# A two-layer graph kernel: column passes of 512 contiguous columns, moving rows laid 544 bytes apart, and other first steps

## The reference

```python
deg = max(sum(adj != 0, axis=-1), 1)
d = rsqrt(deg)
pooled = (d * (adj + I) * d) @ x + x          # layer 0
x = layernorm(x + relu(pooled @ W + b))
# layer 1
a = sigmoid([adj @ x, x] @ Wa.T + ba); g = sigmoid([adj @ x, x] @ Wb.T + bb)
h = x @ W_sa
scores = (h @ a_l)[:, None] + (h @ a_r)[None, :]
e = where(adj != 0, exp(-leaky_relu(scores, 0.01)), 0)
x_a = (e / (sum(e, axis=1) + 1e-5)) @ h
x_b = adj @ (x @ W_gcnb) + b_gcnb
out = layernorm(x + sigmoid(a * x_a + g * x_b))
```

## Time and profile before

| | us |
|---|---|
| median of three runs | 945.04 |
| the profiled execution | 944.09 |
| its span (first to last instruction) | 942.3 |
| PE busy | 901.3 (96%) |
| PE weight loads busy | 783.3 (83%) |
| DVE busy | 640.2 (68%) |
| ACT busy | 459.7 (49%) |
| L1148 / L1031 / L1110 busy on PE | 346.5 / 245.9 / 232.4 |

### The profile page before, as it was taken

The page is one execution under the profiler, slowest core; times in us unless marked ns, Lnnn a source line. Parts: engine busy times, 40 slices in busy tenths (PEclk is TensorE's granted clock), DMA queues, the critical chain, the costliest instruction groups (busy, mean ns, idle before and its releaser), DMA issues.

```text
span 942.3 us, 20464 instructions
## 1 busy us (share of the span) xinstructions
PE 901.3 (96%) x7829; PEld 783.3 (83%) x7829; DVE 640.2 (68%) x1432; ACT 459.7 (49%) x642; POOL 87.4 (9%) x139
## 2 busy tenths in 40 slices
PE   7995799999999999979999999999999999999996
PEld 6874688888888888858888888888888888888885
DVE  6576555544554446777998797797797797797762
ACT  2653455455455324655656365365355455455450
POOL 1020212222212210000000000000000000000000
PEclk8998999999999999979999999999999999999999
DMA  9978899999999400102201110111111211101000
GB/s 303 273 239 266 285 308 329 311 306 338 300 312 332 165 18 18 52 1 74 73 19 68 61 49 35 61 40 44 61 30 54 61 27 56 61 22 59 15 24 12
DMA packets 95784, 121.65 MB, mean 129 GB/s; under 512 B 6480, under 2 KB 91504, under 8 KB 91632
## 3 DMA queue, kind: packets, MB, share of 16 engines
q1 hardware_dynamic: 91120, 116.69, 37.8%
q10 hardware_dynamic: 4608, 4.20, 1.3%
HBM read 95.69 MB, written 25.18 MB: 128 GB/s over the span
## 4 chain that ended last, share of the span: by engine, by line
PE 82%; DVE 9%; ACT 3%; issue 3%; DMA 2%; POOL 0%; SPq 0%; DVEq 0%; ACTq 0%; POOLq 0%
PE ps L1148 32%; PE ps L1031 22%; PE ps L1110 20%; PE ps L1066 4%; DVE ec L866 3%; PE ps L1014 3%; DVE em L875 1%; ACT ec L516 1%; ACT em L519 1%; DMA strip<-in_adj_dram 1%; DMA xs<-in_x_dram 1%; DVE y L640 1%; PE ps L1051 1%; PE ps L1003 1%; DVE codes L600 0%
## 5 line engine op out<-in xcount | busy, mean ns | idle before, releaser
L1148 PE MATMUL ps<-fb,em 128*128 128x257 f16 x3072 | 346.5, 275 | 8.1 <-DVE em L875 8.1
L1148 PEld LDWEIGHTS ps<-fb,em 128*128 128x128 f16 x3072 | 301.4, 98 | 50.9 <-issue 8.6
L1031 PE MATMUL ps<-y,codes 128*128 128x257 f16 x2048 | 245.9, 276 | 11.7 <-DVE lnst L766 7.8
L1031 PEld LDWEIGHTS ps<-y,codes 128*128 128x128 fp8e4 x2048 | 201.8, 99 | 44.9 <-DVE lnst L766 8.1
L1110 PE MATMUL ps<-fa,pan 128*128 128x258 f16 x2048 | 232.4, 273 | 0.9 <-DVE slrow L834 0.9
L1110 PEld LDWEIGHTS ps<-fa,pan 128*128 128x128 fp8e4 x2048 | 199.2, 97 | 30.7 <-DVE slrow L834 1.2
L866 DVE SCALAR_TENSOR_TENSOR ec<-slb,sr,pan 128x256 f32<-128x256 f32 x512 | 207.9, 478 | 7.6 <-issue 7.3
L516 ACT ACTIVATE ec<-ec,sc 128x2048 f32<-128x2048 f32 x64 | 127.9, 1999 | 131.1 <-DVE ec L866 131.1
L875 DVE SCALAR_TENSOR_TENSOR em<-ec,em 128x2048 f16<-128x2048 f32 x64 | 146.4, 2287 | 16.6 <-ACT em L519 16.5
L519 ACT ACTIVATE em<-ec 128x2048 f16<-128x2048 f32 x64 | 122.3, 1911 | 8.2
L738 DVE TENSOR_SCALAR lnst<-ps 128x1 f32<-128x1 f32 x32 | 5.0, 157 | 107.9 <-PE ps L1031 107.9
(11 more groups left out here) (99 smaller groups left out, 503.0 us busy)
## 6 DMA issues: line engine op xcount, KB each, us to landing
strip<-in_adj_dram SPq DMA_DIRECT2D x128, 512.0 KB, 6.2
a_scratch<-codes SPq DMA_DIRECT2D x16, 1024.0 KB, 8.4
pan<-a_scratch SPq DMA_DIRECT2D x16, 1024.0 KB, 5.0
x_scratch<-x ACTq DMA_DIRECT2D x32, 128.0 KB, 4.7
x1r<-x_scratch SPq DMA_DIRECT2D x32, 128.0 KB, 2.1
out_dram<-ot SPq DMA_DIRECT2D x32, 128.0 KB, 1.7
xs<-in_x_dram SPq DMA_DIRECT2D x3, 1024.0 KB, 11.0
slb<-sl_scratch SPq DMA_DIRECT2D x16, 128.0 KB, 4.7
```

What stands on the lines that cost most here:

```text
L1031: mm = pe.matmul(ACC(n), codes[:, qq % SLOTS, h, jb, e * P:(e + 1) * P].bitcast(F8), y[:, jb, part, :], start=(jb == 0 and part == 0), sto ...
L1148: mm = pe.matmul(PH(b)[:, 0:HC], em[slot][:, e_part, jb, (b % 2) * P:(b % 2 + 1) * P], fb[:, jb, h_part, :], start=(jb == 0 and e_part + h ...
```

## The change

What it does:

- A pass takes 512 adjacent columns. A strip is now 2 row blocks of 512 columns (2 KB contiguous) instead of 4 of 256 (1 KB), still 512 KB. `strip_at` and `TILES` go; tiles are taken in the order 0, 1, 2, ... Casts read a strip as it lies and write two pieces of the codes (128x2x2x256 instead of 128x1024). Both code panels of a pass are written to DRAM together.
- xs, fa, zf, fb and y have rows of 272 numbers (`ROW`), so every f16 row begins 544 bytes after the one before; the matmuls still take 257 or 258 columns.
- ACT copies z for the first ten tiles (`ZACT`) and DVE only from the eleventh; DVE takes all six maxima of x and `z_scale` ahead of that. y follows by `split_at`: two tiles a step until it has caught up, then one step behind.
- The weight steps of DVE are spread: `weight_column` at t = 18 to 21, `weight_squares` at 22, `weight_norm` at 26, `weight_scale` at 28, `weight_parts` at 29 and 30.
- 16 row blocks of pass 0 go into the z steps instead of 20 (and 24 before the tile-wise rest: `OUTER`). `t_step(0)` stands behind the third output tile of pass 0 and `p_step(0)` behind the fourth.
- Behind the z steps, ACT and DVE take `head` and `normalize` of the first tiles between the casts, two at a time.
- In the first two panels DVE's `low_chunk` follows its `relu_chunk` by two chunks instead of one, through both panels.

```diff
-SJ = 4
-NSTRIP = NPAN * T // SJ
+SJ = 2
+GS = T // SJ
+NSTRIP = NQ * GS
+ZACT = 10
-YLAG = 10
-OUTER = 24
+OUTER = 16
+ROW = 272
-TILES = [2 * q + h * (T // 2) + e for q in range(NQ) for h in range(2) for e in range(2)]
...
-    fa = at("fa", [P, T, 2, GC], F16, O_X)
+    fa = at("fa", [P, T, 2, ROW], F16, O_X)
-    fb = at("fb", [P, T, 2, HC], F16, O_Z)
-    y = at("y", [P, T, 2, YC], F16, O_Y)
+    fb = at("fb", [P, T, 2, ROW], F16, O_Z)
+    y = at("y", [P, T, 2, ROW], F16, O_Y)
...
-                qq, h, g = strip_at(s)
-                c0 = (qq + h * NQ) * PW
-                sp.dma_start(strip[:, s % RING], adj_view[:, g * SJ:(g + 1) * SJ, c0:c0 + PW]
+                qq, g = s // GS, s % GS
+                sp.dma_start(strip[:, s % RING], adj_view[:, g * SJ:(g + 1) * SJ, qq * 2 * PW:(qq + 1) * 2 * PW]
...
+            return codes[:, s // GS % SLOTS, :, s % GS * SJ:(s % GS + 1) * SJ, :].rearrange("p h j i -> p j h i")
+        strip_of = lambda s: strip[:, s % RING].rearrange("p j (h i) -> p j h i", i=PW)
+        def split_at(t):
+            upto = lambda i: 0 if i < ZACT else min(i - 1, 2 * (i - ZACT) + 2)
+            return range(upto(t - 1), T if t == T else upto(t))
...
             for t in range(T):
                 xt_copy(t)
-                if t >= YLAG:
-                    y_hi(t - YLAG)
-                if 8 <= t < 24 and t % 2 == 0:
+                if 1 <= t <= ZACT:
+                    z_copy(t - 1)
+                for i in split_at(t):
+                    y_hi(i)
+                if 9 <= t < 25 and t % 2 == 1:
                     cast(1)
...
             z_bound()
-            for c in range(4):
+            for c in range(len(XCUT) - 1):
                 x_max(c)
-            for t in range(T):
+            st.sync()
+            dve.tensor_reduce(sc[:, XMX], sc[:, XM], AX, ALU.max).then_inc(S["xmax_part"], 1)
+            z_scale()
+            for t in range(ZACT, T):
                 z_copy(t)
-                if t in (1, 3):
-                    x_max(4 + t // 2)
-                if t == 4:
-                    st.sync()
-                    dve.tensor_reduce(sc[:, XMX], sc[:, XM], AX, ALU.max).then_inc(S["xmax_part"], 1)
-                if t == 5:
-                    z_scale()
-                if t >= YLAG:
-                    y_lo(t - YLAG)
-                if 9 <= t < 25 and t % 2 == 1:
+                for i in split_at(t):
+                    y_lo(i)
+                if 10 <= t < 26 and t % 2 == 0:
                     cast(1)
+                if 18 <= t < 22:
+                    weight_column((t - 18) // 2, t % 2)
                 if t == 22:
-                    weight_columns()
+                    weight_squares()
                 if t == 26:
                     weight_norm()
-                if t == 30:
+                if t == 28:
                     weight_scale()
+                if t in (29, 30):
+                    weight_parts(t - 29)
...
-            cast(6)
-            for n in range(3):
-                head(n)
             cast(2)
+            head(0)
+            cast(2)
+            head(1)
+            cast(2)
+            x1t_lo(0)
+            head(2)
+            cast(2)
+            head(3)
+            parts_lo(0)
+            x1t_lo(1)
...
-            for s in range(2):
-                gate(dve, panel_in[s], 16, "passed_dve")
-                for c in range(NCH):
+            for i in range(2 * NCH + 2):
+                s, c = i // NCH, i % NCH
+                if i < 2 * NCH:
+                    if c == 0:
+                        gate(dve, panel_in[s], 16, "passed_dve")
                     relu_chunk(s, s, c, first=s == 0)
...
-                    if c >= 1:
-                        low_chunk(s, s, c - 1)
-                low_chunk(s, s, NCH - 1)
+                if i >= 2:
+                    low_chunk((i - 2) // NCH, (i - 2) // NCH, (i - 2) % NCH)
...
             for n in range(PT):
-                for jb in range(OUTER, T, SJ):
-                    rows_cast(0, n // 2, jb)
                 sum_rows(n, OUTER, T)
+                if n == 2:
+                    t_step(0)
+            p_step(0)
...
-                    between = {0: ((t_step, 0),), 1: ((p_step, 0), (t_step, 1)), 2: ((p_step, 1),)}
+                    between = {0: ((t_step, 1),), 1: ((p_step, 1),), 2: ((t_step, 2),), 3: ((p_step, 2),)}
                 elif n == PT + 1:
-                    between = {0: ((t_step, 2),), 1: ((p_step, 2), (t_step, 3)), 2: ((p_step, 3),)}
+                    between = {0: ((t_step, 3),), 2: ((p_step, 3),)}
```

More of the change, by code:

```diff
@@ L250, in load_weights, with codes_when_cast @@
                 sp.dma_start(sc[:, BAB.start + 1:BAB.stop], bb.partition_broadcast(P)).then_inc(S["wts_in"], 16)
[L252 to L259, removed]
-                    sp.wait_ge(S[sem], n)
[L261 to L267, removed]
+            def codes_when_cast(qq):
+                for sem, n in zip(("cast_act", "cast_dve"), casts_until(qq * GS + GS - 1)):
+                    sp.wait_ge(S[sem], n)
+                for h in range(2):
+                    sp.dma_start(a8d[2 * qq + h], codes[:, qq % SLOTS, h]).then_inc(codes_out[qq % SLOTS], 16)
             sp.dma_start(xs[:, 0:XCUT[1], 0:D], x_view[:, 0:XCUT[1], :]).then_inc(x_in[0], 16)
@@ L283, in _ @@
                     load_weights()
-                if s >= RING and ends(s - RING):
-                    codes_when_cast(s - RING)
+                if s >= RING and (s - RING) % GS == GS - 1:
+                    codes_when_cast((s - RING) // GS)
             last = (NQ - 3) % SLOTS
@@ L302, in _ @@
                 sp.dma_start(slb[:, m, :], sl0d[m * PW:(m + 1) * PW].partition_broadcast(P)).then_inc(slb_in[m], 16)
-            for s in range(NSTRIP - RING, NSTRIP):
-                if ends(s):
-                    codes_when_cast(s)
+            codes_when_cast(NQ - 1)
             sp.wait_ge(S["slrow_ready"], 1)
@@ L420, in cast @@
                     cast_waits(act, s)
-                    act.activation(codes_of(s), strip[:, s % RING], ACT.Copy, scale=float(EDGE - NONE),
+                    act.activation(codes_of(s), strip_of(s), ACT.Copy, scale=float(EDGE - NONE),
                                    bias=float(NONE)).then_inc(S["cast_act"], 1)
@@ L684, in weight_scale, with weight_parts @@
                 dve.tensor_scalar(sc[:, INVA], sc[:, IAL], 1.0 / EDGE_VAL, None, ALU.mult).then_inc(S["alpha_ready"], 1)
+            def weight_parts(part):
+                st.sync()
+                if part == 0:
+                    st.then(dve.tensor_scalar(wps[:, :, 0, :], wp[:], sc[:, WS], None, ALU.mult))
+                else:
+                    dve.scalar_tensor_tensor(out=wps[:, :, 1, :], in0=wp[:], scalar=sc[:, WS], in1=wps[:, :, 0, :],
+                                             op0=ALU.mult, op1=ALU.subtract).then_inc(S["wps_ready"], 1)
@@ L1104, in a_rows @@
             def a_rows(b, slot, j0, j1):
-                for j in range(j0, j1):
-                    jb = TILES[j]
+                for jb in range(j0, j1):
                     for part in range(2):
                         mm = pe.matmul(PA(b)[:, 0:GC], pan[:, slot, jb, (b % 2) * P:(b % 2 + 1) * P].bitcast(F8),
-                                       fa[:, jb, part, :], start=(j == 0 and part == 0),
-                                       stop=(j == T - 1 and part == 1))
+                                       fa[:, jb, part, 0:GC], start=(jb == 0 and part == 0),
+                                       stop=(jb == T - 1 and part == 1))
                 return mm
```

236 lines of the change are left out of this document (108 added, 128 removed).

## The result

| | before | after |
|---|---|---|
| median of four runs, us | 945.27 | 921.17 |
| the profiled execution, its span | 944.09, 942.3 | 918.60, 916.8 |
| PE busy / DVE busy | 901.3 / 640.2 | 884.7 / 636.0 |
| start of output tile 6 | 122.05 | 106.41 |
| last projection to the third exponential product | 96.3 | 94.1 |

The ratio of the times is 0.9742 (95% interval 0.9721 to 0.9764): 24.1 us gained, where 30.5 were forecast from 945.04, the median of before's first three runs. The profiled execution of after was its fastest run, 2.6 us under its median; that of before lies 1.2 under the 945.27 of the table. So the two traces differ by 25.5 us of span and the medians by 24.1.

The account below looks back on a forecast made before the run. The prediction took PE on the chain (82% of the span) as the bound: matmul pace and PE's waits. Its terms summed to 30.4 us off 945.04, giving 914.5 us, range 905 to 929 (the forecast as told: 908 to 921).

Parts of the forecast that it names:

- A: First steps, up to the start of output tile 6: 14.6 us gained, bounds 21 and 5.
- B: Passes: quicker matmuls of y over 26 tiles, 64 each at 3.2 ns, 5.3 us gained.
- C: First panels: some 78 matmuls of fa ahead of the last projection run quicker, 0.2 us gained.
- D: First panels, new order: 3.0 us gained less 1.5 for a lower clock, so 1.5 us; bounds 3.3 and 0.
- E: Other panels: quicker matmuls of fb (4.8 us) and fa (4.0 us), 8.8 us gained.
- the two terms: The large pace terms B and E, passes and other panels: 14.1 us together, 11.1 by the skill's rule.
- The weights' stall: First steps: DVE idle 4 us ahead of `weight_scale`, waiting for POOL's power; last low part of y at about 68.4.
- the reserve of 1 us: First steps: 1 us added for waits not seen, moving the start of tile 6 from 106.4 to 107.5.
- DMA as the bound: Rival in the passes: DMA too slow for the strips below 322 GB/s, time 953 us; chance 0.05.
- The start gains nothing: Rival in the first steps: late power or lagging strips shrink A to 3, time 926 us; chance 0.09.
- nothing happens: Rival: waits move but their sum stays and the offset does nothing, time 945 us; chance 0.04.
- Half an effect of the offset: Rival on matmul pace: half the row-offset gain, time 922 us; chance 0.14 together with no effect.

Follow-up runs that it names:

- e2: The changed kernel with rows of y, fa and fb packed as before (514, 516, 514 bytes apart), all else kept: 930.7 us, ratio 0.9843.
- e1: The kernel before with only the f16 rows put 544 bytes apart, passes, strips and orders as before: 934.3 us, ratio 0.9896.
- e9: The changed kernel with the low part of each row pair moved up by 8 (y), 4 (fa) and 16 bytes (fb): 920.8 us, ratio 0.9752.
- e3: The changed kernel with rows still 544 bytes apart but starting 2 (y), 4 (fa) and 8 bytes (fb) past a multiple of 32: 922.1 us.
- e4: The changed kernel with rows still 544 bytes apart but starting 16 (y), 8 (fa) and 2 bytes (fb) past a multiple of 32: 922.8 us.
- e7: The changed kernel with the second panel's first two exponential chunks on ACT ahead of the two gate products: 913.9 us, ratio 0.9663.
- e6: The changed kernel with the weights' scale and the two weight parts on DVE behind the last low part of y: 915.8 us, ratio 0.9690.
- e8: The changed kernel with the old order of DVE's low parts in the first two panels: 921.7 us, ratio 0.9754.
- e10: The changed kernel with the old order behind the z steps on DVE and ACT, six casts and then three heads: 923.8 us, ratio 0.9786.
- e12: The changed kernel with rows of y, fa and fb spaced 536, 540 and 530 bytes, leaving 16 or more bytes free: 921.4 us, ratio 0.9746.
- e11: The changed kernel with e6, e7 and, behind the third head, projection and second-x1-tile copies ahead of a cast on ACT and DVE: 902.7 us.

## Why the prediction was right, and where it was not

| term | forecast, us | in the profiles, us |
|---|---|---|
| A, to the start of tile 6 | 14.6 | 15.6 |
| B, 26 tiles | 5.3 | 3.9 |
| C and D, first panels (with the clock) | 1.7 | 0.8 |
| E, other panels | 8.8 | 5.6 |
| the end behind the last product | 0 | -0.4 |
| sum | 30.4 | 25.5 |

(Behind the last product come 7.5 us before and 7.9 after; e2 has the 7.9 too and e1 the 7.5, so they belong to passes and orders. The forecast had them stay.)

*The pace.* The direction was right and the size too large. 26 x 64 matmuls gained 2.4 ns each instead of 3.2; 2688 of fb gained 1.0 instead of 1.8, and 1600 of fa 1.75 instead of 2.5. The step that failed is "after the change every row begins at a multiple of 32, so I take 109.2 for all three lines". In the packed y and fa, 109.2 is the distance from a row at a multiple of 16 to a row that lies elsewhere; e9 shows such short distances paid back by the next one. It is not the pace of an aligned row. Rows at one offset take 110.0 each, at four of the five offsets tried. The rule of the Trainium skill, "TensorE: Matmul & The Clock Gate" (section "Wait — 56ns, not 53.3ns?"), which the prediction set against its own value, gives 109.6 and 110.0 ns. The trace agrees within 0.4 ns (110.0 for both 257 and 258 columns), and by it the two terms were 11.1 us where 9.5 are measured. The cause was mis-stated as well: an effect of the offset, which e3 and e4 exclude for offsets of 4, 8 and 16 bytes. The prediction's own doubt (fb's rows 4 to 12 bytes past ran nearly as fast) pointed there.

*The start.* The sum came out near, and its marks hold in part. First rows at 24.54 (forecast 26, before 29.13); the 4.5 MB of x in the sum are 4096 x 256 x 4 bytes, 4.2 MB. PE's idle time at z step 11 and the two behind it is 1.88 + 0.90 + 0.66 = 3.4 (forecast 4). The weights' stall was there, on DVE 2.18 instead of 4 us, since POOL's power came 7.3 us after its reduction and not 9.2 (from the end of `weight_norm` to `weight_scale` it is 5.2 us, where the sum had 7.3); PE lost 5.58 and the last low part came at 65.9, not 68.4. Pass 0 ended at 82.2 instead of 84.7. Then the second projection waited 2.37 instead of 1.4, and behind it the clock was at its lower level for a while (granted 0.69 in 89.5 to 95 us), so from the end of pass 0 to tile 6 it took 24.3 us instead of 21.7. That the working's own 106.4 came, without the reserve of 1 us, is luck: two misses of 2.5 us of opposite sign. The reading of before was short as well: besides the four waits that it names in the first 125 us, 17.8 us together, PE's timeline has five more, of 0.44, 1.13, 1.67, 1.09 and 0.77.

*The first panels.* Laid out with the old lengths, the waits ahead of the first and third product came as drawn: 2.24 (forecast 2), 4.82 (5), then a product of 22.73 instead of 21.28. The second product came 2.0 us earlier against the last projection, where 2.9 were forecast. By the earlier trace rows and the rows of after, the third product begins 21.8 us earlier. 19.5 of these were gained ahead of the first matmul of fa; 2.3, less 1.5 for the clock, are 0.8 where 1.7 were forecast. e7 shows that ACT's order held the second product: the gate products, which the prediction named as holding back the exponentials.

*What the medians add.* The third product took 22.73 us in after's profile, and 22.8 to 24.3 in the profiles of e2 to e6, e8 to e10 and e12, which wait 4.1 to 5.6 us there, as after does. The granted clock behind that wait, in windows of after and of e9:

```profile
435.00:442.00 7.00, 6.40 (x46) 5.15 (x47) 6.17 (x18) 1.48 (x1) 0.55 (x1) 0.76 0.03 12
```

```profile
436.00:443.00 7.00, 7.00 (x41) 5.21 (x42) 6.26 (x18) 2.00 (x1) 0.55 (x1) 0.62 0.07 20
```

In half microseconds it is one stretch at 0.50 (1.2 GHz) from the product's start, then 1.00 (2.4 GHz). In after:

```profile
438.00:438.50 0.50, 0.50 (x4) 0.37 (x3) 0.50 (x3) 0.00 (x0) 0.00 (x0) 0.50 0.00 0
...
439.00:439.50 0.50, 0.50 (x7) 0.44 (x6) 0.50 (x2) 0.00 (x0) 0.00 (x0) 1.00 0.00 0
```

In e9 the clock is still at 0.50 in 440 to 441 us. So how long it stays low differs between runs: against the same product without a wait (21.28), after's profile lost 1.5 us, e9's 2.6 and e6's 2.8. Whether it falls at all differs too: behind the same wait of 2.2 us the first product took 22.95 in e3, e10 and e11, and 21.5 in after, e6 and e7. That may be the 1.4 us by which the medians' gain falls short of the profiles'; no run isolates it.

*The rivals.* DMA as the bound did not come (0.93 share, PE 50.00 of 50). "The start gains nothing" and "nothing happens" fell with tile 6 at 106.4. "Half an effect of the offset" (922) was the nearest of the rivals: 9.5 of 14.1 us of pace came, and the 921.2 lie at the upper edge of the 908 to 921 that the forecast gave to itself.

## What to carry to other kernels

Lay successive moving rows of a matmul stream at one spacing that is a multiple of 16 bytes (528 and 544 were tried), or at least leave 16 or more bytes between them: here even rows gave 1 to 2.4 ns of 111 to 112 for each of 7168 matmuls, and 9.5 to 11 us. Do not read the fastest single distance in a stream as the pace that all could have; take the mean over a whole period. When a stall goes, look at what stands in front of the next waiting step on each in-order engine: three reorderings gave 16 to 18.5 us more, against the 24.1 of the whole change.

## What was not expected of the hardware

- Even rows take 110.0 ns with 257 and with 258 columns, at offsets of 0, 4, 8 and 16 bytes past a multiple of 32, and at spacings of 528 and 544 bytes. 2 bytes past it they take 110.8 (257 columns).
- Packed rows take 111.0 to 112.4 ns. The same step of offsets with 24 free bytes takes 110.2 (fa).
- POOL's first power after the reduction over partitions starts 7.3 us after the reduction's end in after, 8.6 in e6 and 9.2 before, and 4.6 us after its input was there (54.89) in after. The next power, at 74.27, starts within 0.1 us of its input. The slow one is also POOL's first TENSOR_TENSOR of the execution, and no run tells whether the reduction ahead of it or its being the first makes it late.
- The cast that writes two pieces takes 0.706 us on average, the old one 0.689. By the medians of their 64 casts it is 0.692 and 0.687: single long ones, up to 1.27 us, make most of the difference. The doubled length that the forecast allowed for did not come.
